# Mixture-of-experts outputs scattered with accumulation into two sets of token sums in DRAM

## What is computed

```python
scores = softmax(xf @ Wg)                       # 4096 tokens, 32 experts
weights, indices = top_k(scores, 4)
for e in range(32):                             # tokens that chose e
    out = swiglu(xf[tok], W1[e], W2[e], W3[e]) * w[:, None]
    y = y.at[tok].add(out)                      # four such addends for each token
x = x + y + swiglu(xf, Ws1, Ws2, Ws3)
# then: second cross attention, on layer_norm(x)
```

## Time and profile before

| | us |
|---|---|
| time, median of 3 runs | 1406.05 (1401.76 to 1415.15) |
| the profiled execution, its own time | 1415.33 |
| its span, first to last instruction | 1413.3 |
| first scatter of line 1387 to the last | 518.7 to 799.4 |
| first transfer of `combine` to the first of the second `attend` | 806.3 to 881.9 |

### The profile page before, as it was taken

How to read it: one execution, slowest core, us unless ns; L and a number is a source line. 1 busy time by engine, 2 the same in 40 slices (tenths; PEclk the granted TensorE clock), 3 DMA queues, 4 the chain that set the end, 5 groups by cost and what they waited for, 6 DMA issues and landing times. The chain is left out here.

```text
span 1413.3 us, 27258 instructions
## 1 busy us (share of the span) xinstructions
PE 1212.8 (86%) x8560; PEld 825.7 (58%) x8560; DVE 771.3 (55%) x2028; ACT 518.2 (37%) x1053; POOL 435.9 (31%) x559
## 2 busy tenths in 40 slices
PE   8989999796666359999999537899978999999998
PEld 4457777555444148877778323677764555555554
DVE  3257777656463426656656495688863442443431
ACT  4745555321221014543343136555542222222221
POOL 4321121157667515555555344222200000000000
PEclk9999999787877669999999869999998999999999
DMA  6199100126226355445444291000000000000000
GB/s 165 12 290 390 48 1 1 39 68 113 82 75 224 134 181 152 150 144 169 144 135 140 71 375 55 11 1 1 1 2 0 16 9 7 16 15 15 16 6 25
DMA packets 99296, 123.62 MB, mean 87 GB/s; under 512 B 32688, under 2 KB 74607, under 8 KB 99187
## 3 DMA queue, kind: packets, MB, share of 16 engines
q1 hardware_dynamic: 85363, 87.82, 20.7%
q0 software_dynamic: 13824, 34.38, 6.9%
HBM read 61.62 MB, written 64.72 MB: 89 GB/s over the span
## 5 line engine op out<-in xcount | busy, mean ns | idle before, releaser
L1706 PE MATMUL psA<-H,B 128*128 128x512 f16 x1024 | 223.5, 379 | 0.0
L1631 DVE SCALAR_TENSOR_TENSOR H<-psA,H 128x512 f16<-128x512 f32 x128 | 88.3, 690 | 209.6 <-ACT H L1674 209.6
L1387 POOL DMA_INDIRECT y_rows<-YB,pair x160 | 155.5, 972 | 151.0 <-DVE YB L1442 81.4
L1706 PEld LDWEIGHTS psA<-H,B 128*128 128x128 f16 x1024 | 100.2, 98 | 119.3
L1674 ACT ACTIVATE H<-psA 128x512 f16<-128x512 f32 x128 | 76.4, 597 | 253.7 <-PE psA L1706 253.7
L1497 PE MATMUL psH<-W,XT 128*128 x640 | 168.5, 386 | 1.1 <-issue 1.1
L1087 POOL DMA_INDIRECT x_rows<-XN,slot_s x128 | 131.8, 1029 | 80.3 <-DVE slot_s L1150 41.7
L879 ACT ACTIVATE PHT<-psT 128x512 f16<-128x512 f32 (+1 forms) x192 | 93.5, 521 | 119.2 <-PE psT L939 119.2
L820 DVE TENSOR_REDUCE mx<-psS 128x8 fp32r<-128x616 f32 x128 | 101.6, 795 | 52.3 <-PE psS L918 50.4
L827 DVE TENSOR_TENSOR PLT<-psT,PHT 128x512 f16<-128x512 f32 (+1 forms) x192 | 109.4, 596 | 25.5 <-ACT PHT L879 25.4
L1497 PEld LDWEIGHTS psH<-W,XT 128*128 128x128 f32 x640 | 111.0, 193 | 11.7 <-issue 2.6
(11 more groups left out here) (228 smaller groups left out, 2140.5 us busy)
## 6 DMA issues: line engine op xcount, KB each, us to landing
XG<-x_rows SPq DMA_DIRECT2D x160, 134.0 KB
y_rows<-zero_row SPq DMA_DIRECT2D x4, 4096.0 KB
G<-y_rows SPq DMA_DIRECT2D x7, 2048.0 KB, 10.2
x_rows<-zero_row SPq DMA_DIRECT2D x33, 134.0 KB, 6.5
X<-in_x SPq DMA_DIRECT2D x8, 512.0 KB, 9.0
QT<-in_w SPq DMA_DIRECT2D x1, 4096.0 KB
out_x<-OUT SPq DMA_DIRECT2D x8, 512.0 KB, 2.9
y_rows<-YB,pair POOLq DMA_INDIRECT x160
```

The costliest lines, as they stand in the source:

```text
L1387: pool.indirect_dma_start(y_rows[:, :], bass.IndirectOffsetOnAxis(ap=pair[u // HALF][:, u % HALF:u % HALF + 1], axis=0), YB[u][:], None, b ...
L1631: dve.scalar_tensor_tensor(out=H[layer][1][:, o], in0=psA[k % 4][:], scalar=0.0, in1=H[layer][0][:, o], op0=ALU.max, op1=ALU.subtract).the ...
L1706: last = pe.matmul(psA[k % 4][:], W[:, c, o * P:(o + 1) * P], src[part][:, c], start=n == 0, stop=n == 2 * n_in - 1)
```

## The change

`y_rows` gives way to two arrays of token sums, `y_sums_0` and `y_sums_1`, with 4096 + 128 rows of 256 floats each (8.65 MB together). The pair number becomes the token number. The scatter of tile j adds its rows into array j % 2 (`compute_op=ALU.add`: the DMA reads the destination row, adds and writes it back), and POOL waits before it for the scatter of tile j - 2, which wrote to the same array. Padding rows go to one of 128 spare rows, the partition's own, so every scatter now moves 128 rows; for this `pair` is the smaller of the token number and `spare_row`. The zeroing covers the two arrays with four transfers in runs of 1 KB. `combine` fetches two arrays for each macro (two transfers of 512 KB, into six buffers) and DVE makes two additions in place of four; the split of the first macro into halves is gone.

```diff
-GBUFS = 3
+SUMS = 2
+GBUFS = 6
-    y_rows = nc.dram_tensor("y_rows", (TOKENS * TOPK, D), F32, kind="Internal").ap()
+    y_sums = [nc.dram_tensor(f"y_sums_{k}", (TOKENS + P, D), F32, kind="Internal").ap() for k in range(SUMS)]
-                pool.iota(pair_i[:], pattern=[[P * TOPK, TILES], [1, TOPK]], base=0, channel_multiplier=TOPK)
+                pool.iota(pair_i[:], pattern=[[P, TILES], [0, TOPK]], base=0, channel_multiplier=1)
+                        dve.tensor_scalar(spare_row[:], iota_i[:, EXPERTS:EXPERTS + 1], float(TOKENS), None, ALU.add)
@@ combine, SP @@
-                    sp.dma_start(G[m % GBUFS][:], rows_of(m, 0, MT)).then_inc(fetched[m % GBUFS], 16)
-                for h in range(2):
-                    sp.dma_start(G[0][:, 2 * h:2 * h + 2, :], rows_of(0, 2 * h, 2 * h + 2)).then_inc(halves[h], 16)
+                    for k in range(SUMS):
+                        sp.dma_start(G[m % GBUFS][:, k], y_sums[k][m * MW:(m + 1) * MW, :].rearrange(
+                            "(t p) d -> p t d", p=P)).then_inc(fetched[m % GBUFS], 16)
+                fetch(0)
@@ combine, DVE @@
-                    for k in range(TOPK):
-                        own.done(dve.tensor_tensor(x, x, G[m % GBUFS][:, lo:hi, k * D:(k + 1) * D], ALU.add))
+                    dve.wait_ge(fetched[m % GBUFS], 16 * SUMS * (m // GBUFS + 1))
+                    x = X[:, m * MT:(m + 1) * MT, :]
+                    for k in range(SUMS):
+                        own.done(dve.tensor_tensor(x, x, G[m % GBUFS][:, k], ALU.add))
@@ attend, SP @@
-                    y_flat = y_rows.rearrange("(p n) d -> p (n d)", p=P)
-                    width, n = zero_row[:].shape[1], 16
-                    for i in range(0, TOKENS * TOPK * D // P, n * width):
+                    width, n = zero_row[:].shape[1], 11
+                    size = (TOKENS + P) * D // P
+                    for y in y_sums:
+                        y_flat = y.rearrange("(p n) d -> p (n d)", p=P)
+                        for i in range(0, size, n * width):
+                            part = min(n * width, size - i)
+                            sp.dma_start(y_flat[:, i:i + part].rearrange("p (n w) -> p n w", w=width // 2),
+                                         zero_row[:, 0:width // 2].unsqueeze(1).to_broadcast(
+                                             [P, 2 * part // width, width // 2])).then_inc(y_cleared, 16)
@@ experts, POOL @@
                     pool.wait_ge(y_out, j + 1)
+                    if j >= SUMS:
+                        pool.wait_ge(stored[(j - SUMS) % AHEAD], 16 * ((j - SUMS) // AHEAD + 1))
                     pool.indirect_dma_start(
-                        y_rows[:, :], bass.IndirectOffsetOnAxis(ap=pair[u // HALF][:, u % HALF:u % HALF + 1], axis=0),
-                        YB[u][:], None, bounds_check=TOKENS * TOPK - 1, oob_is_err=False).then_inc(stored[u], 16)
+                        y_sums[j % SUMS][:, :], bass.IndirectOffsetOnAxis(ap=pair[u // HALF][:, u % HALF:u % HALF + 1], axis=0),
+                        YB[u][:], None, bounds_check=TOKENS + P - 1, compute_op=ALU.add).then_inc(stored[u], 16)
@@ experts, meta @@
-                    own.done(dve.tensor_scalar(pair[h][:], to_gate[h][:, :, 0], NOWHERE, None, ALU.add))
+                    own.done(dve.tensor_scalar(pair[h][:], to_gate[h][:, :, 0], NOWHERE, spare_row[:, 0:1], ALU.add,
+                                               ALU.min))
```

More of the change, by code:

```diff
@@ L155, in build @@
     tile_id = always("tile_id", [P, 2])
+    spare_row = always("spare_row", [P, 1])
     minus_half = always("minus_half", [P, MT])
@@ L657, in combine @@
         q = Queries(st, w)
-        G = [space(st, "G", [P, MT, TOPK * D]) for _ in range(GBUFS)]
+        G = [space(st, "G", [P, SUMS, MT, D]) for _ in range(GBUFS)]
         fetched = [sem("fetched") for _ in range(GBUFS)]
-        halves = [sem("halves") for _ in range(2)]
         summed, sum_own = sem("summed"), sem("sum_own")
@@ L666, in _ @@
             def _(sp):
-                def rows_of(m, lo, hi):
-                    return y_rows[(m * MT + lo) * P * TOPK:(m * MT + hi) * P * TOPK, :].rearrange(
-                        "(t p k) d -> p t (k d)", p=P, k=TOPK)
                 def fetch(m):
@@ L688, in _ @@
                 own = Steps(dve, sum_own)
-                def add_up(m, lo, hi):
-                    x = X[:, m * MT + lo:m * MT + hi, :]
-                    for k in range(TOPK):
-                        own.done(dve.tensor_tensor(x, x, G[m % GBUFS][:, lo:hi, k * D:(k + 1) * D], ALU.add))
                 for m in range(MACROS):
-                    if m == 0:
-                        for h in range(2):
-                            dve.wait_ge(halves[h], 16)
-                            add_up(0, 2 * h, 2 * h + 2)
-                    else:
-                        dve.wait_ge(fetched[m % GBUFS], 16 * (m // GBUFS if m % GBUFS == 0 else m // GBUFS + 1))
-                        add_up(m, 0, MT)
+                    dve.wait_ge(fetched[m % GBUFS], 16 * SUMS * (m // GBUFS + 1))
+                    x = X[:, m * MT:(m + 1) * MT, :]
+                    for k in range(SUMS):
+                        own.done(dve.tensor_tensor(x, x, G[m % GBUFS][:, k], ALU.add))
                     dve.sem_inc(summed, 1)
@@ L786, in _ @@
                 if clear_outputs:
-                    y_flat = y_rows.rearrange("(p n) d -> p (n d)", p=P)
-                    width, n = zero_row[:].shape[1], 16
-                    for i in range(0, TOKENS * TOPK * D // P, n * width):
-                        sp.dma_start(y_flat[:, i:i + n * width].rearrange("p (n w) -> p n w", w=width),
-                                     zero_row[:].unsqueeze(1).to_broadcast([P, n, width])).then_inc(y_cleared, 16)
-                    sp.wait_ge(y_cleared, 16 * (TOKENS * TOPK * D // P // (n * width)))
+                    width, n = zero_row[:].shape[1], 11
[7 more added lines that the diff above has]
+                                             [P, 2 * part // width, width // 2])).then_inc(y_cleared, 16)
+                    sp.wait_ge(y_cleared, 16 * SUMS * -(-size // (n * width)))
             @block.gpsimd
```

## The result

| | before | after |
|---|---|---|
| time, median of 4 runs each (us) | 1408.9 (1401.8 to 1415.2) | 1519.8 (1517.0 to 1523.0) |
| ratio | | 1.0797, 95% interval 1.0763 to 1.0830 |
| profiled execution's span | 1413.3 | 1515.2 |
| first scatter of `experts` to the last | 280.7 (518.7 to 799.4) | 404.5 (512.4 to 916.8) |
| `combine`, its first transfer to that of `attend` | 75.6 | 57.8 (924.25 to 982.01) |

The kernel is 8.0% slower, where 1.4% was predicted, and 1519.8 lies above the range. The balance of the two spans (+101.9): `experts` +123.7, from its last scatter to the first fetch of `combine` +0.6 (7.4 or 7.5 us for 6.9), `combine` -17.8, and `experts` begins 6.3 us earlier (512.4 for 518.7). Together +100.2; the rest lies behind `combine`.

A forecast was written before the change was run, and what follows sets the result against it. PE was taken to bound `experts` and DVE `combine`. Scatter loops +36.6, the last landing +1.0 and `combine` -18.5 summed to +19.1 us: median 1406 becomes 1425, range 1388 to 1481.

The forecast's parts named there:

- L: `experts`: loop from one landing through POOL's dispatch, issue and packets to the next, per two tiles; 3.17 us plain, 4.0 adding.
- a: Scatter in `experts`: what accumulation adds to the loop, 0.8 us as two more packet passes of 0.4; bounds nothing to 1.8.
- What bounds the stage: `experts`: PE paces it, scatters 1.765 us apart; two tiles take 3.53 us, against which the new wait is measured.
- Dispatch, 0.77 us: POOL in `experts`: time from a semaphore's release to the scatter's start, 0.77 us of the loop.
- Start to last packet: Plain scatter in `experts`: from its start to its last packet, 1.5 to 1.95 us seen in one place, 2.05 taken.
- rival 4: Scatter in `experts`: POOL's instruction grows too, 0.97 to about 1.9 us; loop about 5.0 us, kernel 1505 us; chance 0.14.
- The size of both together: `experts`, first to last scatter: 79 loops of 4.0 us plus 1.3 give 317.3 us against 280.7, +36.6.
- The extra bytes: DMA engines in `experts`: scatter packets double, load some 0.65 to 0.7, hidden because SP fetches up to eight tiles ahead.
- Landing and rate against the pages: Scatter: one skill page gives 2.6 us for 262 KB, no delay; another says adding halves the rate; neither entered the sum.
- Combine: `combine`: two fewer DVE additions cut the period from 6.96 to 4.6 us; -18.5 us, between -14 and -20.
- Zeroing and `min`: Zeroing, 16.8 to 8.65 MB, lies under the first attention; `min` shares an instruction in `meta`: 0 us.
- The signs: Whole kernel: chance 0.27 of faster by more than about 1%, 0.25 of within 1%, 0.48 of slower.

The follow-up runs named there:

- e6_wait_tags: Kernel before plus only the wait for the scatter two tiles back, SP fetching only the 12 tag and weight columns from the ninth tile: 1381.1 us, ratio 1.015.
- e4_tags_only: Kernel after, with SP fetching only the 12 tag and weight columns from the ninth tile on: 1457.4 us, ratio 1.072 to the kernel before.
- e8_four_sums: Kernel after with four arrays of sums, each scatter waiting four tiles back, four additions in `combine`: 1438.6 us, ratio 1.012 to the kernel before.
- e10_skip_padding: Kernel after with padding rows numbered out of bounds and dropped, no spare rows: 1511.1 us, ratio 1.063 to the kernel before.
- e11_sum_on_pe: Kernel before, scatters untouched; in `combine` PE sums two of four outputs of macros 1 to 7, DVE adds the result: 1411.8 us, ratio 1.002.

## Why the prediction was wrong

The step that failed is the size of L, the loop of an adding scatter: 4.0 us in the forecast, 5.10 on the average in the run. Two terms of it failed: the cost of adding, a, was put at 0.8 and measured 1.3 to 1.35, because the instruction grows as well as the packets; and what disturbs a loop, SP's fetches above all, was put at nothing and measured 0.55. The mechanism, a loop of landings that paces the stage, and the direction were right.

**What bounds the stage** was right: the interval of two tiles is what the loop is measured against. But 3.53 us is a mean; the median of that interval in the kernel before is 3.26, and longer pauses make up the rest. Between the pauses even the plain loop of 3.17 had 0.09 us of slack, not 0.36. With a loop above it the 160 scatters take 79 loops and a step, and `meta`, `y_store` and PE follow them, as the timeline shows.

**Dispatch, 0.77 us**, holds: DVE, which waits for the same landing, starts at 659.12, POOL at 659.80, and the median landing puts the release at 659.05.

**Start to last packet** is the first part that failed. I read 1.95 and 2.05 us from two places and took 2.05 for all, "with the other queue still". The quiet loop of a plain scatter came out right, 3.17 forecast and 3.25 measured (the median of e6_wait_tags). But the path of the loop crosses SP's fetches, which I had put down as hidden since they run eight tiles ahead. They are ahead for PE; for a scatter that shares the 16 engines with them they are in the way. The mean loop of the plain scatter is 3.88: "a plain scatter would not be slowed" is wrong by 45 us on the chip where it was run, where tiles come every 1.65 us. For the chip of the result, with its 1.76, I estimate 307.5 - 280.7 = 27 us from the same stage time; it was not run there.

**The addition, a = 0.8 us**, was too small. Quiet loops went from 3.25 to 4.55 to 4.6, a = 1.3 to 1.35. The instruction brings 0.57 us (1.540 for 0.971; the packets begin 2.1 us after its start where they began 1.5 after it). The packets bring 0.7 to 0.8 (some 1.3 from first to last; the forecast's 2.05 held 0.55 of them), the landing hardly 0.05. I had counted only packets and named the instruction as the upper bound and as rival 4, which is thus half true: it grew by 59%, not by 100%. Against what I chose by, the part "certain to grow" was about the right size, and the part that seemed open came on top. That the size was right is partly luck: the 0.8 was reckoned as two more passes like the one seen, and what the trace has is one packet for each row, 128 of 1 KB in place of 32 of 4 KB.

**The size of both together**: the stage was forecast at 317.3 and took 404.5. Of the 87 us between them 79 x 0.55 = 43 are the quiet loop (4.55 for 4.0) and 43 the disturbed ones (5.10 for 4.55). Of the latter the fetches' volume is some 25, by e4_tags_only. What the rest is, is not shown; e4_tags_only still has 9 loops above 5.9 us where the kernel after has 17. Mean loop 5.10 is what rival 4 gave (L about 5.0, 1505 us), for half of its reason.

**POOL as a bound of its own** is missing in the prediction. 1.84 us a tile is more than the 1.65 to 1.76 that tiles take, and no number of sums mends that: e8_four_sums loses with no waiting left. With POOL's own 1.84 the stage is at least 159 x 1.84 = 293 us on the chip of the result, +12, so I estimate that even a change without any wait would have brought at most -17.8 + 12 = -6 there.

**The extra bytes** were to be hidden. The share of DMA time rose to 0.64 as forecast (0.437 + 0.205 for "0.65 to 0.7"), but over a stage half as long again. Per scatter the queue's time went from 0.165 x 282 / 160 = 0.29 us of all 16 engines to 0.437 x 402 / 160 = 1.10, nearly four times. Without the padding rows' data it is 0.368 x 393 / 160 = 0.90 (e10_skip_padding), so 0.2 of the 1.10 are theirs. PE's wait for XG stayed as it was, so the bytes were hidden from PE, but not from the scatters' own loop. The bytes counted don't show it, 20.96 MB for 16.80.

**Landing and rate against the pages.** The row has 3.8 us from issue to landing for an adding scatter, and 3.3 with half the bytes. By the Trainium skill, DMA: Bandwidth & Descriptors, section "Anatomy of one DMA", 262 KB would land in an estimated 2.6 us: its fit, which agreed for the plain scatter, does not hold here. The packets took some 1.3 us from first to last in place of 0.55. By the Trainium skill, Collectives: The Full Stack, section "The bandwidth ceiling", an add in the DMA path needs two source reads and halves the rate, which the section says of a collective. The trace agrees in direction and shows more than a halving, 1.3 us for 0.55; by the sizes above, the packets were cut smaller as well.

**Combine**: -18.5 forecast, -17.8 and -17.9 measured. The period is 4.44 on DVE for 4.6 expected. **Zeroing and `min`**: nothing on the path, as forecast. The first scatter starts 6.3 us earlier in the kernel after (512.4 for 518.7). It is not the zeroing's: e11_sum_on_pe has the old zeroing and starts at 512.7, beside a kernel before of the same 1408.9 us, and on the chips with 1360 the runs with the new zeroing have it at 478.4 to 481.4 and those with the old at 479.4 to 481.8. Why the profiled run of the kernel before started its scatters late is open. **The end**: +0.6 for +1.0.

**The signs**: slower was the likeliest, and it came. Its size was not foreseen. The range ended at L = 4.7. It had no room for two terms that go the same way: a longer instruction on top of the longer packets (a = 1.35, well inside its own bounds of 0 and 1.8), and 0.55 us of disturbance in the mean loop. Each alone would have stayed within the range (L of 4.55); together they make 5.10.

## What to carry to other kernels

A wait for an earlier transfer turns that transfer's latency into a pace, and then it is the mean latency under all the traffic of the stage that counts, not the one read in a quiet moment: read several loops, among them those in which other queues are at work. When an operation on a DMA changes, price the instruction that issues it as well as its packets, and compare it with the stage's interval before looking at waits: 1.84 us per tile on POOL was already too much here. If results must be accumulated through memory, put the wait three or four back rather than two (three back saved 91 us of stage time here), and compare with what is gained downstream (18 us here, less with every array more).

## What the runs showed of the hardware

- An indirect scatter of 128 rows with an addition takes POOL 1.540 us, a plain one 0.971; the length of the rows (512 B or 1 KB, tried with the addition) doesn't change it. Two on end start 1.84 and 1.27 us apart.
- A plain scatter of 128 rows of 1 KB is 48 packets (32 of 4 KB, 0.168 us each at the median, and 16 small ones), an adding one 144 (128 of 1 KB, 0.102 us each, and 16 small ones). From issue to landing the median is 3.8 us for adding (3.3 with half the bytes) and 3.0 for plain in a stage with fetches; the largest are 7.7 and 6.9.
- The same kernel takes 1359.8 to 1422.5 us on four chips, and its `experts` stage 262.6 to 282.1, while the stage that is bound by the loop of transfers takes 403.7 and 404.5 on two of unlike time.
- Now and then (about every ninth scatter with the fetches gone) a few packets of a scatter come some 1.2 us late. In five such scatters the first late packet starts within 0.01 us of the end of a 16 KB packet of the instruction queue (0.9 to 1.25 us long). No run removes that packet.
